# Block-local attention on one core: the attention stage written out without loops, and one head in sixteen transposed by TensorE

## The reference

```python
x = x + 0.5 * ffn(layernorm(x))       # ternary weights, RMS norm ahead of both linears, gelu
x = x + attention(layernorm(x))       # below
x = x + 0.5 * ffn(layernorm(x))
# attention: 16 heads of 64, blocks of 128 tokens
q, k, v = x Wq / 8, x Wk, x Wv
side    = sums of x over groups of 16 tokens (128 of them), through Wk and Wv
logits  = q . [k, v of the block before, the own block, the block after; side]    # 512 columns
keep |key - query| <= 127; softmax with one extra logit of 0; y = probs . v; out = y Wo
```

## Time and profile before

| | |
|---|---|
| time, median of 3 runs | 2498.21 us (2495.73 to 2502.98) |
| the profiled execution, its own time | 2508.59 us |
| its span | 2506.5 us |
| PE busy | 2198.1 us (88%) |
| PE weight loads busy | 1693.7 us (68%) |
| ACT busy | 2140.6 us (85%) |
| DVE busy | 1893.7 us (76%) |
| POOL busy | 1638.5 us (65%) |
| queue of the transposes and x transfers, share of 16 DMA engines' span | 77.9% |
| mean granted TensorE clock | 0.978 of 2.4 GHz |

### The profile page before, as it was taken

How to read it: one execution, slowest core, us unless ns; L and a number is a source line. 1 busy time by engine, 2 the same in 40 slices (tenths; PEclk the granted TensorE clock), 3 DMA queues, 4 the chain that set the end, 5 groups by cost and what they waited for, 6 DMA issues and landing times. The chain is left out here.

```text
span 2506.5 us, 98603 instructions
## 1 busy us (share of the span) xinstructions
PE 2198.1 (88%) x34394; PEld 1693.7 (68%) x34394; DVE 1893.7 (76%) x4448; ACT 2140.6 (85%) x4422; POOL 1638.5 (65%) x1453
## 2 busy tenths in 40 slices
PE   1888885899899889999988998998899999979998
PEld 0555553677777767777776777777677777746666
DVE  6789986687687767777776876877677777758876
ACT  2988882899899879989987998998799899869998
POOL 1677775577677657767765776776576677647765
PEclk9999996999999999999999999999999999989999
DMA  5100000999999999999999999999999999911001
GB/s 186 49 0 0 0 1 18 144 160 159 146 162 162 160 141 160 160 148 163 163 159 140 161 162 149 162 158 156 144 162 156 158 158 160 157 32 34 33 25 42
DMA packets 1111389, 300.24 MB, mean 120 GB/s; under 512 B 1091440, under 2 KB 1109872, under 8 KB 1110896
## 3 DMA queue, kind: packets, MB, share of 16 engines
q1 hardware_dynamic: 1110896, 294.00, 77.9%
HBM read 14.68 MB, written 8.39 MB: 9 GB/s over the span
## 5 line engine op out<-in xcount | busy, mean ns | idle before, releaser
L987 POOL TENSOR_TENSOR probs_split<-probs,probs_split 128x512 f16<-128x512 f32 (+1 forms) x1026 | 1156.6, 1127 | 578.8 <-ACT probs_split L1267 577.2
L1313 DVE CUSTOM_DVE_ANT_0 score_ps<-score_ps,mask,neg_qk_scale 128x512 f32<-128x512 f32 (+1 forms) x1028 | 750.0, 730 | 337.1 <-PE score_ps L1091 319.8
L1267 ACT ACTIVATE probs_split<-probs 128x512 f16<-128x512 f32 (+1 forms) x1026 | 632.3, 616 | 133.9 <-ACT probs L1252 93.8
L1252 ACT ACTIVATE probs<-score_ps,minus_max 128x512 f32<-128x512 f32 (+1 forms) x1027 | 683.4, 665 | 54.9 <-DVE minus_max L1313 49.4
L1109 PE MATMUL y_ps<-v_parts,probsT 128*128 128x64 f16 x11922 | 520.1, 194 | 96.7 <-DMA probsT<-probs_split 93.3
L1109 PEld LDWEIGHTS y_ps<-v_parts,probsT 128*128 128x128 f16 x11922 | 455.8, 98 | 215.1 <-DMA probsT<-probs_split 157.2
L1088 PE MATMUL score_ps<-k_parts,q_parts 64*128 64x128 f16 (+1 forms) x4524 | 420.7, 235 | 30.7 <-issue 25.1
L1091 PE MATMUL score_ps<-k_parts,q_parts 64*128 64x128 f16 (+1 forms) x4524 | 420.7, 235 | 0.0
L1088 PEld LDWEIGHTS score_ps<-k_parts,q_parts 64*128 64x128 f16 x4524 | 279.2, 94 | 73.9 <-issue 35.8
L1091 PEld LDWEIGHTS score_ps<-k_parts,q_parts 64*128 64x128 f16 x4524 | 279.2, 94 | 0.0
L1020 PE MATMUL item_ps<-b_xT,wk_split 128*128 128x128 f16 x3168 | 223.0, 221 | 13.3 <-DVE b_xT L1305 6.5
(11 more groups left out here) (173 smaller groups left out, 3969.2 us busy)
## 6 DMA issues: line engine op xcount, KB each, us to landing
probsT<-probs_split SPq DMA_TRANSPOSE x1033, 4.1
out_x<-x_resident SPq DMA_DIRECT2D x16, 512.0 KB, 2.9
x_resident<-in_L_attn_x SPq DMA_DIRECT2D x14, 512.0 KB, 4.3
raw_up<-in_L_ffn_w_up SPq DMA_DIRECT2D x1, 1024.0 KB, 5.7
raw_down<-in_L_ffn_w_down SPq DMA_DIRECT2D x1, 1024.0 KB, 7.6
raw_q<-in_L_attn_Wq SPq DMA_DIRECT2D x1, 1024.0 KB, 9.5
raw_k<-in_L_attn_Wk SPq DMA_DIRECT2D x1, 1024.0 KB, 11.5
raw_v<-in_L_attn_Wv SPq DMA_DIRECT2D x1, 1024.0 KB, 13.2
```

The lines of the kernel that those rows point to most:

```text
L987: nc.gpsimd.tensor_tensor(parts_of[v % NPARTS][:, LO, cols], probs[v % NBUF][:, cols], parts_of[v % NPARTS][:, HI, cols], ALU.subtract).th ...
L1252: nc.scalar.activation(probs[v % NBUF][:, cols], score_ps[v % NBUF][:, cols], ACT.Exp, bias=bias[:, j % 2, h:h + 1], scale=-1.0, accum_out ...
L1267: nc.scalar.activation(parts_of[v % NPARTS][:, HI, cols], probs[v % NBUF][:, cols], ACT.Copy).then_inc(phi_done.sem, 1)
L1313: nc.vector.tensor_tensor_reduce(out=score_ps[v % NBUF][:, cols], in0=score_ps[v % NBUF][:, cols], in1=w.mask[:, cols], scale=w.neg_qk_sca ...
```

## The change

**Loops.** The loop over sequences and the loop over inner rounds become Python loops: 16 bodies are written out one behind the other. All awaited values become constants, the register instructions and `separate` go.

**Head 1 of each block.** Its step 4 to 6 (high split on ACT, low split on POOL, DMA transpose) are left out. In their place stands a new item PT1, first in the block's order: in slot 0, behind the values of head 14 of the block before, PE transposes the float32 `probs` of head 1 in four 128 x 128 pieces into `y_ps[0]`. In slot 1 ACT copies the bank as the high part into `probsT[1]`, and DVE subtracts the low part.

**Waits that come with it.** On PE: PT1 waits for the low copy of YT0 of the block before (its bank) and for the exponential of head 1; the values of head 0 wait for the low copy of PT1 (before: for the last item of the block before); the values of head 1 wait for the same instead of a DMA. On ACT: the high copy of PT1 waits until the values of head 13 of the block before have freed `probsT[1]`; the exponential of head 5 waits for PT1's transposes instead of POOL's low split of head 1. SP and POOL go from head 0 to head 2; counts of split and turned heads are by 15 for a block.

```diff
-    V1, Q0, XTR, Q1, K0, YT1, K1, OUTP, YT0, V0 = PLAIN = range(10)
+    PT1, V1, Q0, XTR, Q1, K0, YT1, K1, OUTP, YT0, V0 = PLAIN = range(11)
-    PIECES = [[(V1, 0)], [(V1, 1)], [(Q0, 0)], [(Q0, 1)], [(XTR, 0), (Q1, 0)], [(Q1, 1)], [(K0, 0)], [(K0, 1), (YT1, 0)],
+    PIECES = [[(V1, 0), (PT1, 0)], [(V1, 1)], [(Q0, 0)], [(Q0, 1)], [(XTR, 0), (Q1, 0)], [(Q1, 1)], [(K0, 0)], [(K0, 1), (YT1, 0)],
...
+    BY_PE = {1: PT1}
-    TURNS = (XTR, YT1, YT0)
+    TURNS = (XTR, YT1, YT0, PT1)
...
-        def separate(eng):
-
-            eng.sem_inc(passed, 1)
...
-            with eng.Fori(0, BATCH) as b:
-                body(At(b, 0), b)
-                with eng.Fori(1, ROUNDS - 1) as i:
+            for b in range(BATCH):
+                for i in range(ROUNDS):
                     body(At(b, i), b)
-                body(At(b, ROUNDS - 1), b)
...
             def turn_probs(at, v):
 
-                plo_done.wait(sp, at.heads + v)
-                separate(sp)
+                if v % H in BY_PE:
+                    return
+                plo_done.wait(sp, by_dma(at, v))
                 pv_done.wait(sp, at.heads + v - NBUF)
-                separate(sp)
                 sp.dma_start_transpose(pt[v % NBUF][:], parts_of[v % NPARTS][:].rearrange("p s n -> p (s n)")
                                        ).then_inc(turned[v % NPARTS], 16)
...
+            def turn_probs(at, v, bank):
+
+                exp_done.wait(pe, at.heads + v)
+                for t in range(4):
+                    last = nc.tensor.transpose(bank[:, t * P:(t + 1) * P], probs[v % NBUF][:, t * P:(t + 1) * P],
+                                               w.ident32[:])
                 last.then_inc(item_done, 1)
...
                 if h == 0:
-                    pe.wait_ge(lo_done, at.before(j))
+                    pe.wait_ge(lo_done, at.item(j, PT1) + 1)
                 if h == H // 2:
                     pe.wait_ge(lo_done, at.item(j, YT1) + 1)
-                pe.wait_ge(turned[v % NPARTS], turn_count(at, v))
+                if h in BY_PE:
+                    pe.wait_ge(lo_done, at.item(j, BY_PE[h]) + 1)
+                else:
+                    pe.wait_ge(turned[v % NPARTS], turn_count(at, v))
...
+                if kind == PT1:
+                    pe.wait_ge(lo_done, at.item(j - 1, YT0) + 1)
+                    turn_probs(at, H * j + 1, bank)
+                    return
...
+                if kind in PROBS_TURNS:
+                    waits = [(pv_done.sem, at.heads + H * j + TURNED_HEAD[kind] - NBUF + 1 + pv_done.ahead)]
...
-                separate(act)
-                plo_done.wait(act, at.heads + v - NBUF)
-                separate(act)
+                j_before, h_before = divmod(v - NBUF, H)
+                if h_before in BY_PE:
+                    act.wait_ge(item_done, at.item(j_before, BY_PE[h_before]) + 1)
+                else:
+                    plo_done.wait(act, by_dma(at, v - NBUF))
...
             def split_high(at, v):
 
+                if v % H in BY_PE:
+                    return
                 cols = columns(place_of(at, v))
                 exp_done.wait(act, at.heads + v)
-                separate(act)
                 act.wait_ge(turned[v % NPARTS], turn_count(at, v - NPARTS))
-                separate(act)
```

More of the change, by code:

```diff
@@ L693, in attention_phase @@
 def attention_phase(nc, w):
-    V1, Q0, XTR, Q1, K0, YT1, K1, OUTP, YT0, V0 = PLAIN = range(10)
-    SK0, SK1, SV0, SV1 = range(10, 14)
-    FIRST_ORDER = [SK1, V1, Q0, XTR, Q1, SV1, K0, YT1, K1, OUTP, YT0, V0]
-    LAST_ORDER = [V1, Q0, XTR, Q1, K0, YT1, K1, SK0, OUTP, YT0, V0, SV0]
-    PIECES = [[(V1, 0)], [(V1, 1)], [(Q0, 0)], [(Q0, 1)], [(XTR, 0), (Q1, 0)], [(Q1, 1)], [(K0, 0)], [(K0, 1), (YT1, 0)],
+    PT1, V1, Q0, XTR, Q1, K0, YT1, K1, OUTP, YT0, V0 = PLAIN = range(11)
+    SK0, SK1, SV0, SV1 = range(11, 15)
+    FIRST_ORDER = [SK1, PT1, V1, Q0, XTR, Q1, SV1, K0, YT1, K1, OUTP, YT0, V0]
+    LAST_ORDER = [PT1, V1, Q0, XTR, Q1, K0, YT1, K1, SK0, OUTP, YT0, V0, SV0]
+    PIECES = [[(V1, 0), (PT1, 0)], [(V1, 1)], [(Q0, 0)], [(Q0, 1)], [(XTR, 0), (Q1, 0)], [(Q1, 1)], [(K0, 0)], [(K0, 1), (YT1, 0)],
               [(K1, 0)], [(K1, 1)], [(OUTP, 0)], [(OUTP, 1)], [(OUTP, 2)], [(OUTP, 3)],
@@ L727, in attention_phase @@
     LAST_SIDE = {9: SK0, 15: SV0}
-    TURNS = (XTR, YT1, YT0)
+    BY_PE = {1: PT1}
+    TURNS = (XTR, YT1, YT0, PT1)
     KEYS, QUERIES, VALUES = (K0, K1, SK0, SK1), (Q0, Q1), (V0, V1, SV0, SV1)
     SECOND = (K1, Q1, V1, SK1, SV1, YT1)
-    N_PIECES = {k: 1 if k in TURNS else 4 if k == OUTP else 2 for k in range(14)}
+    N_PIECES = {k: 1 if k in TURNS else 4 if k == OUTP else 2 for k in range(15)}
+    TURNED_HEAD = {kind: h for h, kind in BY_PE.items()}
+    PROBS_TURNS = tuple(BY_PE.values())
     NI = len(PLAIN)
@@ L811, in attention_phase @@
         y_cleared = sem("y_cleared")
-        passed = sem("b_passed")
         block = ctx.enter_context(nc.Block())
-        def separate(eng):
-            eng.sem_inc(passed, 1)
         class At:
@@ L825, in __init__ @@
                 self.heads = self.round * U
-                self.eights = self.round * (U // NPARTS)
+                self.splits = self.round * (RING * (H - len(BY_PE)))
                 self.halves = self.round * (2 * RING)
@@ L859, in place @@
                 if kind in TURNS:
-                    return y_ps[int(kind != YT0)], None
+                    return y_ps[int(kind in (XTR, YT1))], None
                 prefix = LAST_ORDER if self.first else [*PLAIN]
@@ L873, in __init__ @@
                 self.heads, self.halves, self.blocks = NBLK * H, NBLK * 2, NBLK
-                self.eights = NBLK * H // NPARTS
+                self.splits = NBLK * (H - len(BY_PE))
                 self.items = PRE_ITEMS + 4 * BATCH + NI * NBLK
@@ L896, in finished @@
             side = side_item(at, j, h)
-            return [(j, k) for k, piece in PIECES[h] if piece == N_PIECES[k] - 1] + ([(j, side)] if side else [])
+            pieces = [(j, k) for k, piece in PIECES[h] if piece == N_PIECES[k] - 1]
+            if side == SK1:
+                return [(j, side), *pieces]
+            return pieces + ([(j, side)] if side else [])
         def due(at, u):
@@ L941, in turn_count, with by_dma @@
         def turn_count(at, v):
-            return (at.eights + v // NPARTS + 2) * 16
+            j, h = divmod(v, H)
+            n = v % NPARTS
+            each = sum(k not in BY_PE for k in range(n, H, NPARTS))
+            return (at.blocks * each + j * each + sum(k not in BY_PE for k in range(n, h + 1, NPARTS)) + 1) * 16
+        def by_dma(at, v):
+            j, h = divmod(v, H)
+            return at.splits + j * (H - len(BY_PE)) + sum(k not in BY_PE for k in range(h))
         def half(v):
@@ L983, in split_low @@
             def split_low(at, v):
+                if v % H in BY_PE:
+                    return
                 cols = columns(place_of(at, v))
-                phi_done.wait(pool, at.heads + v)
+                phi_done.wait(pool, by_dma(at, v))
                 nc.gpsimd.tensor_tensor(parts_of[v % NPARTS][:, LO, cols], probs[v % NBUF][:, cols],
@@ L1047, in turn_x @@
                 last.then_inc(item_done, 1)
+            def turn_probs(at, v, bank):
[3 more added lines that the diff above has]
+                                               w.ident32[:])
+                last.then_inc(item_done, 1)
             def turn_y(h, e):
@@ L1170, in body @@
                     for kind, piece in PIECES[h]:
-                        if kind in (YT0, YT1):
+                        if kind in (YT0, YT1, *PROBS_TURNS):
                             block_item(at, b, j, kind, (piece,))
@@ L1193, in destination @@
                 return xt[xt_parity][:, :, part, :]
+            if kind in PROBS_TURNS:
+                return pt[TURNED_HEAD[kind] % NBUF][:, 4 * part:4 * part + 4, :]
             if kind in KEYS:
@@ L1204, in result @@
                 return bank[:, 0:KD * P].rearrange("p (k n) -> p k n", k=KD)
-            return bank[:].rearrange("p (c n) -> p c n", c=4) if kind in (YT0, YT1) else bank[:]
+            return bank[:].rearrange("p (c n) -> p c n", c=4) if kind in (YT0, YT1, *PROBS_TURNS) else bank[:]
         def ring_slot(j, kind):
@@ L1311, in largest @@
                 scores_done.wait(dve, at.heads + v)
-                separate(dve)
                 nc.vector.tensor_tensor_reduce(out=score_ps[v % NBUF][:, cols], in0=score_ps[v % NBUF][:, cols],
```

## The result

The changed kernel takes 2389.94 us (median of 4 runs, 2389.93 to 2393.72) beside 2497.86 for the kernel before: 0.9569 of it, 95% interval 0.9552 to 0.9586, so 108 us or 4.3% faster. The forecast was 2369, in a range of 2312 to 2436. The profiled execution took 2389.95 us.

A forecast was written before the change was run, and what follows sets the result against it. SP and its transposes bound the kernel before; afterwards ACT and PE jointly, 25.3 us a block. 38 (pauses) + 87 (blocks) + 4 (edge blocks) = 129 us off 2508.6, less 10.4: 2369 us, range 2312 to 2436.

The forecast's parts named there:

- the last step of the sum: From the forecast profiled execution of 2379.6 us, 10.4 us subtracted because the median of the runs lies below it: 2369 us.
- Pauses, term 38 us: Attention stage: seven pauses at loop jumps go when written out, slow aftermath partly; 38 us gained, between 26 and 46.
- My 46: The attention stage's 1752 us less 1706 us of steady work, 64 x 26.66: 46 us counted as something else.
- SP, 1.49 to 1.35 us: SP's short transpose cycle loses register update and increments; 15 issues a block then take 23.1 us, at worst 25.2.
- ACT, increments 5 x 0.08 us: On ACT, five bare waits a block lose two increments each: 0.4 us saved, bounds 0 and 0.15 each.
- PE, 24.5 us a block: PE's work: 24.4 us plus 0.5 for four transposes, less part of the score-pair gaps; range 24.0 to 24.9.
- My deduction of 0.4 us: On PE, part of eight gaps of about 0.2 us behind score pairs goes with the register work: 24.9 to 24.5.
- The new waits: PE's waits for YT0 and PT1 copies, covered by 1.0 and 0.7 us: cost nothing, up to 0.5 us per block.
- Together, 25.3 us a block: ACT 24.7 and PE 24.5 bound jointly, SP 23.1 behind, 0.6 us lost to coupling; 64 x (26.66 - 25.3) = 87 us.
- the relief of SP (15 issues for 16): SP issues 15 transposes a block instead of 16, part of its fall from 26.66 to 23.1 us.
- My rivals: SP and DMA pace 2367 (0.17); coupling 2436 (0.15); ACT alone 2312 (0.08); exposed PT1 trip 2648 (0.06); pauses stay 2462 (0.04).

The follow-up runs named there:

- Head 9: The changed kernel with head 9 of each block turned by PE too, in the second y bank: 2468.3 us, 0.9879 of the kernel before.

## Why the prediction was right, and where its sum was off

**The whole.** 108 us came of 129, so the direction and the range held, and the forecast was 21 us too low. Half of the difference is the last step of the sum. The profiled execution of before lay 10.4 us above the median, and I subtracted the same from the forecast; the profiled execution of the changed kernel lies at its median. By profiled executions the forecast was 2379.6 and the measurement 2389.95, 119 us of 129. An offset of one run of the kernel before is no property of the changed one.

**Pauses, term 38 us.** The loops alone gave 62 us by medians. Between the profiled executions the stages lie 77 us apart and the times 73 (the rest lies outside the stage), and 11 us of that is by how much the profiled execution of before stood above its median. Of the 77, 35 to 46 are pauses, depending on the stretch taken as steady, and the others a shorter SP cycle. So the term of 38 was sized well. My 46 took a fast stretch for the steady one: part of it was slower work elsewhere in the stage, not pauses.

**SP, 1.49 to 1.35 us.** 1.38 measured by the three in a row. It left the bound, as forecast, and rests 174 us in the stage instead of 67. The instruction fetches stayed: 254 packets of q8 instead of 269.

**ACT, increments 5 x 0.08 us.** The most undersized term, even beyond its bound of 0.15. 0.17 of the 0.20 us goes. In the trace the split now carries the wait for the exponential itself, where before a separate record with the wait and the increment stood in front of it. With 53 us (no PE transposes) and 57 us (with them) the increments are half of the gain, 0.8 to 0.9 us a block; in the changed kernel ACT's share is 33 to 43 us and SP's 11 to 21.

**PE, 24.5 us a block.** From one score pair to that 16 slots later, an undisturbed block (its windows view first); with it head 1's transposes, its two copies and the next PE step:

```profile
1399.99:1424.98 24.99, 24.86 (x486) 20.79 (x484) 21.76 (x54) 24.22 (x60) 17.86 (x16) 1.00 1.05 160
...
1399.99 0.23 PE L1105 MATMUL score_ps<-k_parts,q_parts 64*128 64x128 f16 x1
...
1400.76 0.84 PE L1029 MATMUL item_ps<-b_xT,wq_split 128*128 128x128 f16 x12
...
1423.41 0.63 PE L1062 MATMUL y_ps<-ident,probs 128*128 128x128 f32 x4
...
1423.88 0.81 PE L1029 MATMUL item_ps<-wv_split,b_xT 128*128 128x512 f16 x3
...
1424.08 0.61 ACT L1247 ACTIVATE probsT<-y_ps 128x512 f16<-128x512 f32 x1
...
1424.73 0.69 DVE L1335 TENSOR_TENSOR probsT<-y_ps,probsT 128x512 f16<-128x512 f32 x1
...
1424.98 0.23 PE L1105 MATMUL score_ps<-k_parts,q_parts 64*128 64x128 f16 x1
```

1424.98 - 1399.99 = 24.99 us, just above the top of my 24.0 to 24.9. It is PE's own sum but for one wait of 0.4 us for DVE: PE is busy 24.86 us of it, and the weight loads have no other wait over 0.15 us than "issue". The gap behind the score pairs hardly shrank with the register instructions: 68 us "issue" before projections, 77 us before, and a step of 0.77 us where the earlier trace rows has 0.76. My deduction of 0.4 us failed. The four transposes take 0.47 us until the next step, as costed; the 275 ns each of the Trainium skill (TensorE: Matmul & The Clock Gate, Part 4: PE-mode transpose) hold for the single instruction here as well, whose median is 273 ns (float32 here, bfloat16 on the page), but four of them overlap.

**The new waits.** Cost next to nothing, as forecast: PE's weight loads wait 0.8 us in all for yT copies, ACT 4.4 us for the transposes. With the transposes done at 1424.04 and the low copy at 1425.42 the trip takes 1.4 us of the 2.5. Head 9 shows what a missing slot would have cost: it is 78 us in all, of which 64 x 0.47 = 30 us are the four more transposes themselves.

**Together, 25.3 us a block.** 25.5 measured. Right as a number, for partly wrong reasons: ACT saved more than I gave it and the coupling took more; that the two nearly cancel is luck. ACT's own sum is now about 25.8 - 0.05 - 0.6 - 5 x 0.17 = 24.3 us, PE's 24.6 to 25.0, SP's 15 x 1.38 + 2.8 = 23.5, and yet 25.5 pass. Taking 0.86 us from PE or ACT, or 1.35 from SP, gave 0 to 20 us in all, where a lone bound would have given 55 to 86. What remains is waiting of the engines for each other: ACT for DVE's maxima 73.5 us, PE for transposes 40 us, DVE for scores 171 us. That it is the ring exponential, scores, maximum, exponential, with in-order work in between, is argued and not shown.

**The part that the change is named for.** The step that failed is in how I divided the gain: it took the relief of SP (15 issues for 16) as part of what lets the period fall. Written out and without increments, SP with 16 transposes needs 16 x 1.38 + 2.8 = 24.9 us by the same sum, under the 25.4 that this kernel reaches (16 x 1.587), and PE has 0.47 us less to do. So turning head 1 on PE made the kernel slower in all three comparisons: by 6 and 7 us without increments, and by 11 us with them. The whole gain came from the loops (62 us) and the increments (53 us). My rivals had no case for it.

## What to carry to other kernels

When a change has parts that can be separated, cost each against the period that the other parts leave, not against the kernel before: here the transposes relieved a queue that the other two parts had already relieved. A wait that can ride on the instruction it guards is cheaper than one followed by something else: here 0.17 us at five places of a block on ACT was worth more than a whole moved step. Where three engines stand within some 6% of each other, don't give an engine's trimmed time its full value in the sum: here it was a fifth to two fifths for PE, a sixth at most for ACT and an eighth for SP.

## What the runs showed of the hardware

One 16 KB instruction fetch holds the transposes for about 1.2 us. It does so in the loops and in straight code, as the DMA view of the changed kernel shows, 1313 to 1317 us in 40 slices, around an issue of 2.09 us:

```profile
GB/s 172 174 103 133 205 233 215 195 218 195 218 376 200 166 139 149 85 54 10 5 8 8 8 10 10 10 10 8 10 205 287 287 292 179 233 287 292 287 298 138
...
q8 instruction: 1, 0.02, 1.5%
```

In the attention stage of the changed kernel 243 such packets were fetched, and the transposes fell below 30 GB/s for 0.8 us or longer 241 times, 1.2 us in the median; in the kernel before it was 255 packets and 241 times. A loop's jump back cost 35 / 7 = 5.0 to 46 / 7 = 6.6 us in this kernel, all told, on all engines at once: in the 8 us of the first pause PE was busy 3.75 us and ACT 3.08. TensorE's granted clock fell there: 0.69 in the mean of that window, so part of it at 1.2 GHz instead of 2.4. At the last pause, 5 us long, it stayed at 1.00, and in the straight code it is 1.00 through the stretch. The Trainium skill (Runtime: NRT & Kernel Launch, Instruction fetch mechanics) names the jump; it calls the crossing of a fetch block mostly hidden, and for the engine that fetches it may be, but the transfers beside it are held up, as the row shows.
